# A six-layer local-attention stack: the score and mix series of matmuls taken apart into three parts each

## The reference, cut to what matters

```
DIM, DEPTH, HEADS, DIM_HEAD, WINDOW = 128, 6, 16, 64, 32
def attn_layer(x, Wqkv, qs, ksc, Wo):
    q, k, v = split_heads(x @ Wqkv)                 # 16 heads of 64
    q, k = l2norm(q) * qs, l2norm(k) * ksc
    q, k = rotary(q), rotary(k)                     # cos, sin and a scale by position
    sim = einsum('bhwie,bhwje->bhwij', q, look(k)) * 8.0   # windows of 32, and the window before
    attn = softmax(where(mask, -max, sim))
    return merge_heads(einsum('bhwij,bhwje->bhwie', attn, look(v))) @ Wo
def ffn_layer(x, g, bln, W1, b1, W2, b2):
    a, gate = split((layernorm(x) * g + bln) @ W1 + b1)    # 2 x 341
    return a * gelu(gate) @ W2 + b2
for i in range(DEPTH):
    x = attn_layer(shift_tokens(x), ...) + x
    x = ffn_layer(shift_tokens(x), ...) + x
```

## Time and profile before

| what | value |
| --- | --- |
| time, median of 3 runs | 2190.03 us (2189.59 to 2193.81) |
| the profiled execution's own time | 2187.69 us |
| its span | 2185.9 us |
| PE busy | 1743.0 us, 80% |
| DVE busy | 1350.5 us, 62% |
| ACT busy | 894.3 us, 41% |
| mean granted clock of PE | 0.891 |
| the stack, from the first mask (709.7) to the last (1622.35) | 912.65 us, 47 steps |

### The profile page before, as it was taken

How to read it: one execution, slowest core, us unless ns; L and a number is a source line. 1 busy time by engine, 2 the same in 40 slices (tenths; PEclk the granted TensorE clock), 3 DMA queues, 4 the chain that set the end, 5 groups by cost and what they waited for, 6 DMA issues and landing times. The chain is left out here.

```text
span 2185.9 us, 47509 instructions
## 1 busy us (share of the span) xinstructions
PE 1743.0 (80%) x20107; PEld 1085.1 (50%) x20107; DVE 1350.5 (62%) x2406; ACT 894.3 (41%) x1609; POOL 635.3 (29%) x994
## 2 busy tenths in 40 slices
PE   2005167699776889898898888999887999999999
PEld 1002045443443556555565556555554677676433
DVE  5796746421275878788778777788663556554311
ACT  1001023233223555556456455556553454553332
POOL 0000012000023756666557556656630000000000
PEclk6556579699798999999999999999896999999799
DMA  1000000001004343333334333333311000000100
GB/s 31 21 0 11 1 26 10 15 29 29 27 0 120 108 115 89 102 102 94 103 96 107 89 96 99 98 88 86 89 29 39 1 1 1 1 1 1 30 29 29
DMA packets 66259, 111.70 MB, mean 51 GB/s; under 512 B 9936, under 2 KB 29238, under 8 KB 66050
## 3 DMA queue, kind: packets, MB, share of 16 engines
q1 hardware_dynamic: 65234, 108.44, 18.3%
q10 hardware_dynamic: 816, 0.24, 0.0%
HBM read 82.14 MB, written 26.03 MB: 49 GB/s over the span
## 5 line engine op out<-in xcount | busy, mean ns | idle before, releaser
L1319 POOL TENSOR_TENSOR st_r<-st_r,st_t 128x512 f32<-128x512 f32 x192 | 243.3, 1270 | 295.2 <-DVE st_t L1286 295.0
L1243 PE MATMUL PS<-st_wqkv,st_xs 128*128 128x512 f32 x576 | 311.1, 625 | 16.6 <-DVE st_xs L1496 9.1
L1334 POOL TENSOR_TENSOR st_r<-st_r,st_gy 128x512 f32<-128x512 f32 x192 | 198.7, 1065 | 3.8
L1278 DVE TENSOR_TENSOR st_r<-PS,st_rot 128x512 f32<-128x512 f32 x192 | 129.8, 676 | 107.9 <-ACT st_sqh L1262 107.3
L2035 ACT ACTIVATE la_p<-PS,la_nmx 128x589 f32<-128x589 f32 x128 | 95.0, 747 | 133.5 <-DVE la_nmx L2066 133.5
L2066 DVE TENSOR_REDUCE la_nmx<-PS 128x1 f32<-128x589 f32 x128 | 92.7, 766 | 91.8 <-PE PS L1928 91.8
L1262 ACT ACTIVATE st_sqh<-PS 128x512 f32<-128x512 f32 x192 | 114.3, 595 | 73.5 <-PE PS L1243 73.3
L1063 DVE TENSOR_TENSOR m_y<-PS,m_wb 128x512 f32<-128x512 f32 x32 | 22.1, 691 | 187.7 <-ACT m_wb L1036 187.7
L641 POOL MEMSET l_s<- 128x144 f32 x2 | 0.5, 225 | 459.8 <-DVE x L531 270.0
L1346 PE MATMUL PS<-cst,st_r 128*128 128x128 f32 x768 | 119.2, 290 | 16.0 <-issue 11.6
L1286 DVE TENSOR_TENSOR st_t<-PS,st_rot 128x512 f32<-128x512 f32 x192 | 130.4, 679 | 0.0
(11 more groups left out here) (315 smaller groups left out, 3677.0 us busy)
## 6 DMA issues: line engine op xcount, KB each, us to landing
st_vv<-st_v_out SPq DMA_DIRECT2D x168, 256.0 KB, 4.8
st_v_out<-st_v SPq DMA_DIRECT2D x48, 512.0 KB, 2.6
st_wqkv<-in_st_wqkv SPq DMA_DIRECT2D x18, 512.0 KB, 7.5
m_w<-in_m_w SPq DMA_DIRECT2D x32, 256.0 KB, 3.0
st_vv<-st_v_out SPq DMA_DIRECT2D x24, 192.0 KB, 3.3
st_wo<-in_st_wo SPq DMA_DIRECT2D x6, 512.0 KB
st_w<-in_st_w SPq DMA_DIRECT2D x6, 341.0 KB
la_wc<-in_la_wc SPq DMA_DIRECT2D x1, 1344.0 KB, 6.4
```

The lines of the kernel that those rows point to most:

```text
L1243: pe.matmul(PS[:, 2 + m % 2, :], self.xs[:, b, P * t:P * t + P], self.wqkv[:, l % 2, k, 512 * half:512 * half + 512], start=True, stop=Tru ...
L1278: dve.tensor_tensor(h3(self.r[:, t % 2, c, :]), h3(ps), self.rot[:, k, 0, t, :].unsqueeze(1) .broadcast_to([P, 8, D2]), ALU.mult)
L1319: pool.tensor_tensor(r, r, self.t2[:, c % 2, :], ALU.add).then_inc(self.added, 1)
L1334: pool.tensor_tensor(r, r, y[:, 8 * c:8 * c + 8].unsqueeze(2).broadcast_to([P, 8, D2]), ALU.mult)\
```

## The change

`pe_scores` and `pe_mix` get an argument `pairs` that says which of the eight pairs of heads they do, and the mask matmuls become a function of their own, `pe_mask`. PE's order then puts other work between the parts. In the scores it is the first turn of o and projection piece 0; in the mix it is turn 1 of r and projection piece 4. The turned pieces are those that stood right behind the series before. The signals `scores` and `pv_done` still go out once, with the last matmul. In the norm step, `pe_var` stands behind the whole mix and in front of turns 2 and 3, `pe_spread` behind these, `act_ln_root` behind ACT's `act_proj` 4, and `dve_ln_root` behind `dve_proj` 2. No work is added or removed.

```diff
-        def pe_scores(self, pe, T):
-            t = T % self.TILES
+        def pe_mask(self, pe, T):
             pe.wait_ge(self.r_evac, 4 * T + 4)
             if T > 0:
                 pe.wait_ge(self.on_ready, T)
...
-            for c in range(8):
+        def pe_scores(self, pe, T, pairs):
+            t = T % self.TILES
+            for c in pairs:
...
-            mm.then_inc(self.scores, 1)
+            if c == 7:
+                mm.then_inc(self.scores, 1)
...
-        def pe_mix(self, pe, T):
+        def pe_mix(self, pe, T, pairs):
...
-            for c in range(8):
+            for c in pairs:
...
-            mm.then_inc(self.pv_done, 1)
+            if c == 7:
+                mm.then_inc(self.pv_done, 1)
...
                 if here:
-                    self.pe_scores(pe, T)
+                    self.pe_mask(pe, T)
+                    self.pe_scores(pe, T, range(0, 3))
                 if past:
                     self.pe_turn_o(pe, T - 1, 0)
+                if here:
+                    self.pe_scores(pe, T, range(3, 6))
                 if lead:
                     self.pe_proj(pe, T + 2, 0)
+                if here:
+                    self.pe_scores(pe, T, range(6, 8))
                 if past:
                     self.pe_turn_o(pe, T - 1, 1)
...
                 if here:
-                    self.pe_mix(pe, T)
+                    self.pe_mix(pe, T, range(0, 3))
+                if turn:
+                    self.pe_turn_r(pe, T + 1, 1)
+                if here:
+                    self.pe_mix(pe, T, range(3, 6))
+                if lead:
+                    self.pe_proj(pe, T + 2, 4)
+                if here:
+                    self.pe_mix(pe, T, range(6, 8))
                 if norm_of is not None:
                     self.pe_var(pe, norm_of)
-                if turn:
-                    self.pe_turn_r(pe, T + 1, 1)
-                if lead:
-                    self.pe_proj(pe, T + 2, 4)
-                if norm_of is not None:
-                    self.pe_spread(pe, norm_of)
                 if end_of is not None:
                     self.pe_up(pe, end_of, 2)
                 if turn:
                     self.pe_turn_r(pe, T + 1, 2)
                     self.pe_turn_r(pe, T + 1, 3)
+                if norm_of is not None:
+                    self.pe_spread(pe, norm_of)
...
                 if lead:
                     self.dve_proj(dve, T + 2, 2)
                 if norm_of is not None:
+                    self.dve_ln_root(dve, norm_of)
                     self.dve_ln_out(dve, norm_of)
```

More of the change, by code:

```diff
@@ L1365, in pe_scores @@
                 pe.matmul(PS[:, e, :], self.identb[:, :],
-                          self.wmask[:, min(t, 1), :].unsqueeze(1).broadcast_to([P, 8, 2 * WIN]),
+                          self.wmask[:, min(T % self.TILES, 1), :].unsqueeze(1).broadcast_to([P, 8, 2 * WIN]),
                           start=True, stop=False, skip_group_check=True)
-            for c in range(8):
+        def pe_scores(self, pe, T, pairs):
+            t = T % self.TILES
+            for c in pairs:
                 for w in range(4):
@@ L1678, in act @@
                     self.act_turn_r(act, T + 1, 0)
-                if norm_of is not None:
-                    self.act_ln_root(act, norm_of)
                 if end_of is not None:
@@ L1686, in act @@
                     self.act_proj(act, T + 2, 4)
+                if norm_of is not None:
+                    self.act_ln_root(act, norm_of)
                 if end_of is not None:
@@ L1729, in dve @@
                     self.dve_out(dve, T)
-                if norm_of is not None:
-                    self.dve_ln_root(dve, norm_of)
                 if lead:
```

## The result

The changed kernel takes 2197.24 us (median of 20 runs, 2190.56 to 2200.90), the kernel before 2187.74 us (20 runs, 2176.97 to 2193.81). The ratio is 1.0049, with a 95% interval of 1.0035 to 1.0063: about 10.7 us slower, where 10 us faster was forecast. The profiled execution took 2194.09 us, with a span of 2192.3 us.

What follows compares the result with a forecast made beforehand. PE was taken to be bound by work plus waits for late instruction pieces behind the loads of v. Shorter waits -50 us, breaks and delays +41, so -9 on a median of 2190: 2180 us forecast, range 2158 to 2212.

Steps and rivals of the forecast that it cites:

- What bounds the kernel, and the fetch: In the stack PE counts, and starves when 16 KB instruction pieces come late behind the loads of v; waits 52.5 us.
- The waits: PE's instruction waits in the stack fall from 52.5 to about 22 us: mix and turns 18 less, scores 16.4 to 5.
- The factor of 1.58: Each microsecond of PE's waits costs 1.58, since 52.5 us of waits cost 83 with the slower clock behind them.
- The breaks: Parting the scores and mix costs 0.5 us a series; 14.51 step to about 15.2, plain steps +0.4 and +0.6.
- The norm step: Later mix end delays the reciprocal, so pe_spread waits 1.5 us for st_rs; step 18.9 against 17.51, +1.4 us.
- The up step: Later mix end delays pe_down by 0.8 us, with a PE gap of 0.4; with 0.4 from the scores, +1.2 us.
- The clock: PE's granted clock over the stack was to be above 0.97; the listed costs had no clock term.
- The sum: Whole kernel: gain of 50 us against cost of 41, so 9 us faster; cost 3.6 us a group of four steps.
- the rivals: Slower, waits only move with the loads of v: 0.24; faster, waits nearly vanish: 0.18; no gain, not fetch waits: 0.08.
- the 0.3 for slower: Chance 0.30 of slower by over 4.4 us: 0.02 from the forecast, 0.20 lateness stays, 0.08 no fetch waits.

Runs made afterwards that it cites:

- run with thin loads: Kernel before, with loads of v bringing only 32 of 512 columns after the first sequence: 2140.34 us, ratio 0.9789 to the kernel before.
- changed order with thin loads: Changed kernel, with loads of v bringing only 32 of 512 columns after the first sequence: 2170.06 us, ratio 0.9934 to the kernel before.
- kernel with late loads: Kernel before, with the loads of v held until the next step's scores are done by one added wait on SP: 2140.92 us, ratio 0.9806.

## Why the prediction was wrong

Time and waits of the profiled executions can be put together. The kernel before and its run with thin loads have the same order; their stacks differ by 912.65 - 868.25 = 44.4 us and their waits by 35.4 us, so a microsecond of waiting costs 1.25, the slower clock behind it included. Without waits that order would take 868.25 - 27.0 = 841.2 us. The changed order with thin loads takes 889.25 with 0.8 us of waits, so the change costs 889.25 - 1.0 - 841.2 = 47.0 us. This gives the changed kernel 841.2 + 47.0 + 26.7 x 1.25 = 921.6 us, where 920.48 was measured, and the kernel with late loads 868.2, where 865.05 was. These are single executions. Costs taken from the medians instead come out higher (29.7 us between the thin runs, at 1.37 a microsecond 58); which of them is nearer is left open.

The single steps give the 841 a second time, and show part of the 47. First come an undisturbed plain step of the kernel before and an undisturbed norm step of its run with thin loads, each behind an undisturbed step. Then two norm steps of the changed kernel with thin loads, neither with a wait for instructions, and PE's last rows in the longer of these.

```profile
1152.43:1167.31 14.88, 14.46 (x318) 9.81 (x319) 13.33 (x21) 8.17 (x14) 11.97 (x20) 1.00 0.41 108
...
1452.29:1470.30 18.01, 16.90 (x334) 11.45 (x333) 16.57 (x28) 13.01 (x23) 13.39 (x22) 1.00 0.11 36
...
1235.49:1254.61 19.12, 17.75 (x333) 11.77 (x333) 16.28 (x27) 12.94 (x22) 13.46 (x21) 1.00 0.29 89
1158.17:1178.53 20.36, 18.99 (x333) 12.35 (x333) 16.85 (x28) 12.94 (x22) 13.46 (x21) 0.94 0.09 31
...
1175.94 1.08 PE L1544 MATMUL PS<-cst,st_rs 128*128 128x128 f32 x4 [1.37 <-DVE st_rs L1539]
1176.83 1.91 PE L1244 MATMUL PS<-st_wqkv,st_xs 128*128 128x512 f32 x2
```

- **What bounds the kernel, and the fetch.** Right. Pieces of instructions that come late are what PE waits for, and the loads of v make 35 of the 57 us. The prediction named only these loads; 21.6 us stay without them.
- **The waits.** Forecast: 30 us less. Measured: 57.0 to 26.7, 30.3 less, the longest 2.5. The total was right with some luck, for its parts were not: the scores lost 5.6 us and not 11, the mix and the turns 22.5 and not 18.
- **The factor of 1.58. This step failed.** I had summed undisturbed steps to 830 us, called the other 83 us the cost of the waits, and divided by 52.5. The sum was too low. The plain step of 14.51 and the norm step of 17.51 each stand right behind a step with one of the longest waits (3.96 and 3.69 us). Behind undisturbed steps the plain one takes 14.88, and the norm step 18.0 in the runs with thin and with late loads. That the other engines caught up during the wait is argued, with one sign for it: in the 17.51 `pe_spread` waits 0.19 us for `st_rs`, in others up to 0.96. With 18.0, 23.58, 16.3 and 14.88 a group takes 72.8 us and not 71.9. With first steps of 60 us in all and not 58, the stack without waits is some 841 us. So the waits, 57.0 us on all lines, cost 71 us and not 83, which is 1.25 each. The gain was 30.3 x 1.25 = 38 us and not 50.
- **The breaks.** Forecast +0.5 us a series, measured +0.62. I had priced the way out of small tiles by the turn behind a series (0.06); into a projection piece it is 0.1, and the earlier trace rows have no projection piece behind a series. The last plain step became 15.47 or 15.40 and not 15.2. In the two others the forecast of +0.4 was too high (+0.35 and -0.28); why one of them got shorter, no run shows. The Trainium skill (TensorEngine Tiling (Array Packing), Key Properties) has the rule that a change of tiling mode drains TensorE. The trace agrees that the changes cost time: with the same matmuls, PE is busy 842.5 us against 797.6 in the two runs with thin loads, 0.24 us for each of the 188 added breaks. That it is a drain, no run here shows.
- **The norm step.** The wait for `st_rs` is 1.37 where I had 1.5, and the step takes 19.12 where I had 18.9. Against 17.51 that is +1.6, for a forecast of +1.4; against the 18.0 of other undisturbed steps it is only +1.1.
- **The up step. Too small.** Forecast +1.2, measured +1.9. The runs with one series parted show 0.8 for the scores, where I had 0.4, and 1.1 for the mix, where I had 0.8. In the timelines the maximum on DVE now waits for the scores, and the exponential, the table load, the square and the gate stand behind it in a row. From the mix to `pe_down` are 7.26 us (1368.85 to 1376.11), 1.04 more than the 6.22 of before. The wait before `pe_down` is 0.24 and not 0.4.
- **The clock, a cost put at nothing.** In three of the 11 norm steps of the changed kernel with thin loads, PE runs at the 1.2 GHz level behind the wait for `st_rs`: 1.91 us for the projection piece of the step of 20.36, where 1.02 is usual. The three take 20.11 to 20.36 us and not 19.12, and the up steps behind them 25.9 to 26.0 and not 25.45: 5 us in all, with no wait for instructions.
- **The sum.** From undisturbed steps to undisturbed steps the change costs 1.1 + 1.9 + 0.03 + 0.55 = 3.6 us a group, some 42 us in the stack, near the 41 of the forecast. That is luck: I had put a group of the changed kernel 0.8 us too low (75.5 for 76.3) and one of the kernel before 0.9. With the 5 us of the clock it is 47, as from the totals. -38 + 47 = +9, against -50 + 41 = -9; the stacks differ by 7.8, the medians by 9.5.

The forecast knew both terms and had them opposed. Its sum was a small difference of two numbers near 45. By the stacks the gain was 12 us less and the cost 6 us more, both to the same side; by the medians the cost has the larger part in it. None of the rivals is what happened: the waits shrank as much as forecast, did not vanish, and are fetch waits. What decided, that a wait is worth less than it seemed while the breaks and delays are paid in full, had no rival of its own; so the 0.3 for slower had the wrong reasons in it.

## What to carry to other kernels

- Where an engine waits for its own instructions, look first at what the DMA queues carry at that time. Moving four loads of 256 KB a step by about half a step with one wait gave 48 us; parting the matmuls, which takes away nearly as much waiting, cost more than it gave.
- Don't divide the distance to the best steps by the waits to get the price of a wait: the best steps may be those behind the longest waits. Take steps that stand behind undisturbed ones, or run the kernel with the cause taken away and read the price from the two.
- A series of small matmuls in three parts costs 0.6 us, and everything behind its last matmul moves by the work that was put within. Ask for each kind of step what waits for that last matmul.

## What the runs showed of the hardware that I had not expected

- Instruction fetch can be what limits PE, even with nearly idle DMA engines: 21.6 us of waits stayed at a DMA share of 0.16, with 256 instructions in 1.42 us, and one of 1.82 us stood where the engines had been busy 0.3% in the 6 us ahead of the fetch. With 3.3 us for the same series and its insertions, 0.8 us are left. The Trainium skill (Runtime: NRT & Kernel Launch, Instruction fetch mechanics) says that instructions come in blocks of 16 KB and that their fetch is hidden by the rate at which they are issued. The traces agree on the 16 KB and not on the second: 57.0 us of waits here were not hidden.
- Of small matmuls that follow each other, the first 22 start within 0.21 us. A part of 48 or 32 behind other work begins each time at about this rate: 0.72 and 0.45 us from the first start to the last end, of which one matmul takes 0.21. Three parts then start their matmuls in 2 x 0.51 + 0.24 = 1.26 us, as one series does in 1.27. So they lose nothing within themselves; the whole cost is at their ends.
- All 11 norm steps of the changed kernel with thin loads have the wait of 1.37 us for another engine. Behind it PE is at the lower clock level in three of them (granted clock 0.94 to 0.95 over the step) and stays at the higher in the others, though each of the three stands behind a step at 1.00. What decides it, no run shows.
